# Six subtractions of an input split on GpSimd instead of VectorE, in a chain of four convolution blocks on one Trainium2 core

## The reference, cut to what matters

```
x: (16, 32, 28, 28) f32                       # NCHW
h = relu6(bn(conv1x1(x, ternarize(w1))))      # 32 -> 192 channels
h = relu6(bn(conv3x3(h, ternarize(w2))))      # 192 -> 192, padding 1
x = x + bn(conv1x1(h, ternarize(w3)))         # 192 -> 32
# L1: two 3x3 convolutions, 32 -> 32, on activations and weights rounded to 8 bits
#     (scale = the largest value of the whole tensor / 255 or / 127), bn, relu, + identity
# L2, L3: conv3x3 32 -> 32, bias, bn, relu; channels whose maximum is under 1e-3 become 0
```

## Time and profile before

| | us |
|---|---|
| median of 3 runs | 293.54 (293.44 to 294.15) |
| profiled execution, its own time | 295.54 |
| its span, first to last instruction | 293.7 |
| PE busy | 248.8 (85%) |
| DVE busy | 252.3 (86%) |
| ACT busy | 195.0 (66%) |
| POOL busy | 11.7 (4%) |
| mean granted TensorE clock | 0.967 |

### The profile page before, as it was taken

How to read it: one execution, slowest core, us unless ns; L and a number is a source line. 1 busy time by engine, 2 the same in 40 slices (tenths; PEclk the granted TensorE clock), 3 DMA queues, 4 the chain that set the end, 5 groups by cost and what they waited for, 6 DMA issues and landing times.

```text
span 293.7 us, 5676 instructions
## 1 busy us (share of the span) xinstructions
PE 248.8 (85%) x2138; PEld 135.3 (46%) x2138; DVE 252.3 (86%) x480; ACT 195.0 (66%) x287; POOL 11.7 (4%) x24
## 2 busy tenths in 40 slices
PE   1174959798999999999999999999779999496873
PEld 0131425354555555555555555555335555253432
DVE  6489997999999999988999998995678589898973
ACT  3577766587777578666677859785227389659753
POOL 6500000000000000000000000000000000000111
PEclk9999999899999999999999999999999999777978
DMA  7933002121100000000000000000000000503232
GB/s 180 261 91 76 6 9 71 34 56 46 36 2 1 2 0 3 0 2 0 0 0 0 0 0 0 3 0 2 0 2 0 0 3 1 111 18 65 83 93 109
DMA packets 5654, 10.05 MB, mean 34 GB/s; under 512 B 1728, under 2 KB 3968, under 8 KB 5632
## 3 DMA queue, kind: packets, MB, share of 16 engines
q1 hardware_dynamic: 5360, 9.27, 12.2%
q10 hardware_dynamic: 272, 0.49, 0.8%
HBM read 4.04 MB, written 1.61 MB: 19 GB/s over the span
## 4 chain that ended last, share of the span: by engine, by line
PE 61%; DVE 21%; ACT 7%; issue 5%; DMA 4%; SPq 0%; DVEq 0%; ACTq 0%
PE ps L428 14%; PE ps L418 14%; PE ps L449 8%; PE ps L571 7%; PE ps L438 7%; PE ps L395 3%; DMA big<-w2a_in 3%; PE ps L603 3%; DVE big L1274 2%; PE ps L464 2%; ACT big L835 2%; PE ps L511 1%; DMA big<-big 1%; DVE ug L994 1%; DVE part L1313 1%
## 5 line engine op out<-in xcount | busy, mean ns | idle before, releaser
L664 ACT ACTIVATE ra<-ps,bn 128x392 f32<-128x392 f32 x64 | 43.2, 675 | 28.6 <-PE ps L395 26.0
L686 ACT ACTIVATE hs<-ug,magic 128x784 f16<-128x784 f16 x32 | 30.2, 948 | 18.1 <-DVE ug L994 18.1
L603 PE MATMUL ps<-big,wst 128*32 128x392 f16 (+2 forms) x576 | 31.1, 383 | 10.0 <-ACT vv L848 6.5
L428 PE MATMUL ps<-vv,w2at 128*128 128x392 f16 x192 | 38.5, 334 | 0.3 <-DVE ps L1028 0.3
L418 PE MATMUL ps<-vv,wu 128*128 128x392 f16 x180 | 37.1, 341 | 0.0
L395 PE MATMUL ps<-xk,w1t 96*128 (+1 forms) x60 | 21.0, 349 | 12.6 <-ACT ra L664 12.6
L603 PEld LDWEIGHTS ps<-big,wst 128*32 128x32 f16 x576 | 17.8, 109 | 23.3 <-issue 9.5
L835 ACT COPY big<-part 32x900 f16<-32x900 f16 x24 | 22.6, 940 | 9.1 <-DVE part L1301 5.4
L571 PE MATMUL ps<-qi,wqi 128*128 128x392 bf16 x144 | 25.0, 333 | 1.0 <-ACT qi L799 1.0
L428 PEld LDWEIGHTS ps<-vv,w2at 128*128 128x128 f16 x192 | 18.3, 97 | 13.8 <-issue 1.2
L418 PEld LDWEIGHTS ps<-vv,wu 128*128 128x128 f16 x180 | 17.7, 98 | 12.7 <-issue 1.1
(11 more groups left out here) (213 smaller groups left out, 468.9 us busy)
## 6 DMA issues: line engine op xcount, KB each, us to landing
xk<-xpart SPq DMA_DIRECT2D x45, 49.0 KB, 1.9
big<-big SPq DMA_DIRECT2D x4, 450.0 KB, 3.8
xin<-x_in SPq DMA_DIRECT2D x4, 392.0 KB, 9.9
y_out<-xin SPq DMA_DIRECT2D x3, 392.0 KB, 2.4
big<-w2a_in SPq DMA_DIRECT2D x3, 288.0 KB, 5.7
big<-w2b_in ACTq DMA_DIRECT2D x1, 432.0 KB, 7.4
big<-w2b_in SPq DMA_DIRECT2D x1, 432.0 KB, 9.6
y_out<-xin SPq DMA_DIRECT2D x2, 196.0 KB, 2.0
```

Of the source, the lines that this page charges most:

```text
L428: i = nc.tensor.matmul(ps[:, PBANK[k], :HALF], weights(s, k, dx, False), moving(s, k, dx, b), start=False, stop=(s == 2 and dx == 2), skip ...
L603: i = nc.tensor.matmul(ps[C * g:C * g + C, bank + h, :W * (rows.stop - rows.start)], wst[:, layer, C * t:C * t + C], kst[:, layer, c % 2, ...
L664: nc.scalar.activation(dst[:, HALF * h:HALF * h + HALF], ps[:, bank, :HALF], ACT.Relu, bias=bn[:, BSH, at:at + 1], scale=bn[:, BSC, at:at ...
L686: nc.scalar.activation(inner(hs[:, 2 * two]), img(ug[:, two, :]), ACT.Identity, bias=magic[:, 2:3]).then_inc(hh_ready, 1)
```

## The change

The splits of chunks 1, 2 and 3 move from DVE's queue to POOL's, behind the identity matrix; the split of chunk 0 stays on DVE and is written out. The two instructions and their semaphores are the same, the waits too, with two added: chunk c waits for `x_split` of the chunk before, and chunk 1 for `expb_done` of image 0, since the matmuls of image 0 read `xrest`. ACT, SP and PE are untouched.

```diff
@@ gpsimd
+            ptt = nc.gpsimd.tensor_tensor
+            for c in range(1, NCH):
+                pool.wait_ge(s_x[c], 16)
+                pool.wait_ge(xc_ready, c)
+                pool.wait_ge(x_split, c)
+                if c == 1:
+                    pool.wait_ge(expb_done, 2)
+                if c >= 2:
+                    pool.wait_ge(s_ximg1, 48)
+                    pool.wait_ge(s_xk[c - 2], XK[c - 2])
+                ptt(xrest[:], xin[:, c, :], high(xin[:, c, :]), ALU.subtract).then_inc(xr_ready, 1)
+                pool.wait_ge(xr_ready, c + 1)
+                ptt(xpart[:, c % 2, 2, :], xrest[:], high(xrest[:]), ALU.subtract).then_inc(x_split, 1)
@@ vector
-            def split(c):
...
-            split(0)
+            dve.wait_ge(s_x[0], 16)
+            tt(xrest[:], xin[:, 0, :], high(xin[:, 0, :]), ALU.subtract).then_inc(xr_ready, 1)
+            dve.wait_ge(xr_ready, 1)
+            tt(xpart[:, 0, 2, :], xrest[:], high(xrest[:]), ALU.subtract).then_inc(x_split, 1)
...
             rows_12(1, 1)
-            split(1)
             slot(0, 0, first=True)
-            split(2)
...
             slot(0, 1, first=True)
-            split(3)
```

## The result

The changed kernel takes 294.83 us (median of 20 runs), the one before 293.46 us (20 runs, the three shown ahead among them): ratio 1.005, 95% interval 1.0031 to 1.0069, so +1.4 us, with an interval of 0.9 to 2.0 us. The direction was the forecast's, the size about half of it (+2.94 us forecast).

The account below looks back on a forecast made before the run. DVE was taken as the bound before about 62 us. Pushes of 2.58, 1.84 and 2.30 us less 3.79 us taken off gave +2.94 us on 293.54, so 296.5 us; forecast range 293.0 to 298.5, with rivals 289.5 to 299.0.

Parts of the forecast that it names:

- The bound, and what is taken away: DVE bounds the kernel before about 62 us; the splits of chunks 1 and 2 on that path give 3.79 us.
- Exclusion: Each POOL subtraction keeps a DVE instruction that draws two streams out for its whole length; +2.94 us, chance 0.56.
- Rival 1: POOL and DVE do not disturb each other, so the 3.79 us are gained: 289.7 us; chance 0.26.
- Rival 2: Partial disturbance, engines taking turns within an instruction or DVE's queue mostly winning: 293.1 us, 291 to 295; chance 0.12.
- Rival 2's other half: DVE's back-to-back queue mostly wins and POOL slips into DVE's idle, 2.33 us of 40 to 53 us.
- Rival 3: POOL's subtraction takes twice the estimate, 3.28 us, still exclusive: 306 us; chance 0.06.
- the pushes in the sum: Delays of DVE by POOL's subtractions for chunks 1, 2 and 3: 2.58, 1.84 and 2.30 us.
- the price of a subtraction: One two-input subtraction of 784 elements on POOL: 0.20 + 2 x 0.72 = 1.64 us, ends 0.97 and 1.84.
- Chunk 1, 2.58 predicted: From 19.0 us, POOL's first subtraction pushes L994 by 0.94 us; the second goes ahead of L952, 1.64 more.
- Chunk 2, 1.84 predicted: First subtraction gets in before rows_03, +1.64 us; second runs beside seed_pair and scales, pushing L1128 by 0.2 us.
- Chunk 3, 2.30 predicted: From about 56.7 us, the first subtraction keeps L1017 out 1.15 us, the second L1042 another 1.15 us.
- the +4.1 us given for it: Result if a subtraction on POOL takes 1.84 us, with pushes of 2.98, 2.2 and 2.7 us.

Follow-up runs that it names:

- e3: The changed kernel with only chunk 3's split on POOL, the other splits back on DVE: 294.31 us against 293.64 for the kernel before.
- e7: Splits of chunks 1 and 2 on POOL, all four subtractions placed by waits on DVE's progress, chunk 3 on DVE: 290.64 us against 293.66 for the kernel before.
- e4: All splits stay on DVE as in the kernel before; POOL adds six subtractions into unused memory: 298.29 us against 293.64.
- e1: The changed kernel with only chunk 1's split on POOL, the other splits back on DVE: 294.1 us against 293.64 for the kernel before.
- e5: All splits on DVE; POOL adds six memsets of 1740 words, which only write, instead of spare subtractions: 294.66 us against 293.66 for the kernel before.
- e2: The changed kernel with only chunk 2's split on POOL, the other splits back on DVE: 293.11 us against 293.64 for the kernel before.
- e6: Only chunk 2's split on POOL, its second subtraction waiting until rows_12 of slot 0 is done: 291.87 us against 293.66 for the kernel before.

## Why the prediction was right in its mechanism and wrong in its size

**The bound, and what is taken away: right.** The chain leaves DVE before chunk 3's split, each of the first two splits was worth its 1.89 and 1.90 us (L1022 starts at 40.46 where rows_12 ends, the reductions at 52.66), and ACT's waits went without a further gain. Chunk 3's split brings nothing when it leaves DVE and only costs: in e3 PE comes 0.85 us later, with 0.82 us of pushes. That PE can follow a faster DVE by more than the 1.12 us before 68.84 is shown by e7, 2.93 us earlier.

**Exclusion: right, and shown.** e4 puts the six instructions beside DVE and takes nothing away: +4.7 us. Rival 1, no disturbance, would have 0 there, and -1.9 us in e1. Rival 2's turn-taking within an instruction is out, since a few instructions carry the whole delay and their neighbours none. The time alone could not tell, since 294.83 us lies in rival 2's 291 to 295. Rival 2's other half, that DVE's back-to-back queue wins, came true in part: L1022 went ahead of a waiting POOL at 40.46, and POOL's first subtraction of chunk 2 then cost nothing. Rival 3 falls by 1.49 us.

**The step that failed is the size of the pushes in the sum: all three terms were too large, first by the price of a subtraction, then by the order and the overlap.** Predicted pushes were 2.58 + 1.84 + 2.30 = 6.72 us; measured are 2.02 + 1.17 + 2.12 = 5.31 us, and some 0.09 us more came in at the L999 of 48.53, which waits 0.95 us for ACT instead of 0.86. 5.40 - 3.79 = 1.61 us.

- The price of a subtraction. The estimate of two full streams (0.20 + 2 x 0.72 = 1.64 us) was 0.15 us too high; it is 1.49 us. The Trainium skill's "GPSIMD Engine Reference", section 3.1, with its 2.6 cycles an element, gave the estimate of 1.70 us and is further off.
- Chunk 1, 2.58 predicted and 2.02 measured (L972 at 21.31 after an L999 at 17.96; 21.03 after 19.70 before). The places were right. POOL had started 0.57 us ahead of L999, which was pushed 0.78 instead of 0.94; the second subtraction was over at 20.66 and L957 had been started at 19.23, so it waited 1.43 us, of which 0.20 us passed for its own time too: 1.23 us, not the whole length. That overlap lowers every push, and I had not counted it.
- Chunk 2, 1.84 predicted and 1.17 measured. This is the chunk with the largest error, 0.67 us: 0.28 of it is the price, the rest the order and the overlap. I let POOL's first go in ahead of rows_03. DVE's L1022 started 0.18 us after POOL's was issued and still went first (POOL's is recorded at 2.98 us). The first subtraction then fell beside seed_pair and scales, where I had put the second, and cost nothing; only the second met the two-column product.
- Chunk 3, 2.30 predicted and 2.12 measured. Again DVE's L1022 was first, and the pushes fell on L1047 (0.82) and L999 (1.28). That this total came out near is luck: the price was too high, and what the pushes fell on was wrong.

Had POOL been priced at 1.49 us in my own order, chunk 1 would be 0.79 + 1.49, chunk 2 1.49 + 0.07 and chunk 3 about 2 x 1.0, 5.8 us in all and +2.0 us at the end. The price explains about 0.9 us of the 1.3 us by which I missed the trace's 1.61; the order and the overlap explain the rest.

The stated range has an error of its own: its upper end of 298.5 us does not follow from the +4.1 us given for it, which is 297.6.

**Still open.** What decides who goes first when both stand ready. At 40.3 us POOL's request was 0.18 us older than L1022, and L1022 went first, behind a two-input instruction. At 19.2 and 57.4 us POOL's request was 0.27 and 0.26 us older than L957 and L999, and POOL went first, behind a one-input instruction that takes 0.57 us for 784 elements (L999) or 0.56 us (L1047). That the kind of the running instruction decides it is a guess from one case on one side; nothing was made to test it. What decides between forms in e5 is likewise known only for the forms that were met. Whether the lower clock of PE in slot 0 of the profiled execution (mean granted clock 0.77 from 40 to 53 us, 1.00 before) caused the 0.09 us was not tried either.

## What to carry to other kernels

In this kernel, work moved from VectorE to GpSimd was priced by what VectorE did at that moment, not by GpSimd's idle share: four placed instructions cost 0.8 us and four unplaced ones 3.2 us. Put GpSimd's elementwise work beside reductions, reads of PSUM or idle, with a wait on VectorE's own progress, and leave on VectorE what lies behind the path (chunk 3). When forecasting, walk the instruction list and let GpSimd's request wait for the instruction in flight first; and compare traces from a common instruction, as the start of an execution moved by up to 2.3 us here (L994 at 17.45 us in e4, 19.70 before).

## What the runs showed of the hardware that I had not expected

- Length does not matter to the one kept out: a `TENSOR_SCALAR` on two columns (0.23 us alone) took 1.40 us beside a subtraction of 1.49 us.
- A one-input reduction, a reciprocal on two columns and instructions with one input in PSUM run beside GpSimd's reads at their usual 0.44, 0.17 and 0.56 us.
- The exclusion was at work in the kernel before already, in a row that the prediction read as the nearest against it. GpSimd's power of 9 elements takes 1.83 us in e2, e3 and e6, where it starts after VectorE's second subtraction of chunk 0 is over. It is recorded with 2.39 us before and 2.50 us after, where it starts earlier, and ends 1.69 and 1.70 us after that subtraction. So some 0.6 us of it is GpSimd waiting for VectorE. One trace alone could not show this.
- The power does not keep VectorE's two copies out once it runs: they take 0.45 us inside it. So a hold does not seem to last as long as the instruction is open. That is argued, not tested, and whether copies of this form can be kept out at all is not known.

The power and the copies in the kernel after, then the power in e2:

```profile
9.15 2.50 POOL L344 TENSOR_TENSOR bn<-bn,expo 128x9 f32<-128x9 f32 x1
```
```profile
9.98 0.45 DVE L937 COPY w1t<-w1t 32x256 bf16<-32x256 bf16 x2
```
```profile
10.46 1.83 POOL L344 TENSOR_TENSOR bn<-bn,expo 128x9 f32<-128x9 f32 x1
```
